# T1 = W22 - W12 formed by TensorE with an identity and a negated identity, in an f32 kernel of 64 conditioned 64x64 mixings and a routed 1024x1024 layer

## The reference

```python
W = weights[condition]
y = jnp.einsum('bct,bcd->bdt', x, W)
logits = y @ gate_w.T + expert_bias
one_hot = jax.nn.one_hot(jnp.argmax(logits, axis=-1), 4)
base_out = jnp.einsum('bth,oh->bto', y, W_up)
z = jnp.einsum('nh,erh->ner', y, lora_A)
d = jnp.einsum('ner,ehr->neh', z, lora_B)
out = x + base_out + jnp.einsum('neh,ne->nh', d, one_hot)
```

## Time and profile before

| | value |
|---|---|
| median of 3 runs | 405.35 us (405.1 to 405.51) |
| the profiled execution's own time | 405.92 us |
| its span in the trace | 404.1 us |
| TensorE (PE) busy | 398.5 us, 99% |
| VectorE (DVE) busy | 300.8 us, 74% |
| ScalarE (ACT) busy | 110.3 us, 27% |
| GpSimd (POOL) busy | 129.1 us, 32% |
| granted TensorE clock | 1.0 in the profile's row |

### The profile page before, as it was taken

The page is one execution under the profiler, slowest core; times in us unless marked ns, Lnnn a source line. Parts: engine busy times, 40 slices in busy tenths (PEclk is TensorE's granted clock), DMA queues, the critical chain, the costliest instruction groups (busy, mean ns, idle before and its releaser), DMA issues.

```text
span 404.1 us, 9748 instructions
## 1 busy us (share of the span) xinstructions
PE 398.5 (99%) x3451; PEld 358.3 (89%) x3451; DVE 300.8 (74%) x719; ACT 110.3 (27%) x226; POOL 129.1 (32%) x121
## 2 busy tenths in 40 slices
PE   8899999999999999999999999999999999999997
PEld 8899988989888898988979798898988889898996
DVE  3899668889876859676696766867677766967775
ACT  5896211323114031312213130130311203131310
POOL 1687302529031350505205080221605043050710
PEclk9999999999999999999999999999999999999999
DMA  7910330503214123413125032150332221250102
GB/s 255 350 62 2 122 101 28 190 27 113 87 66 145 53 87 105 133 55 113 50 78 187 28 109 68 49 177 26 110 104 93 95 79 58 104 182 27 54 32 99
DMA packets 20993, 39.39 MB, mean 97 GB/s; under 512 B 7494, under 2 KB 7750, under 8 KB 20970
## 3 DMA queue, kind: packets, MB, share of 16 engines
q1 hardware_dynamic: 17600, 27.40, 18.9%
q10 hardware_dynamic: 3370, 11.69, 9.3%
HBM read 22.30 MB, written 16.78 MB: 97 GB/s over the span
## 4 chain that ended last, share of the span: by engine, by line
PE 96%; DMA 1%; SPq 1%; ACT 1%; issue 0%; DVE 0%
PE bank_y L878 23%; PE bank_x L878 22%; PE bank_b L878 11%; PE bank_c L929 10%; PE y_ps L791 7%; PE bank_c L1083 5%; PE bank_b L1083 4%; PE bank_x L856 2%; DMA cond_pair<-in_L_cond_weights_dram 1%; PE bank_c L878 1%; PE bank_b L884 1%; PE bank_x L884 1%; PE bank_y L884 1%; PE bank_c L884 1%; PE bank_y L856 1%; PE y_ps L1157 1%
## 5 line engine op out<-in xcount | busy, mean ns | idle before, releaser
L878 PE MATMUL bank_y<-w_s,hl_s 128*128 128x292 f32 (+1 forms) x384 | 51.5, 290 | 0.0
L878 PEld LDWEIGHTS bank_y<-w_s,hl_s 128*128 128x128 f32 x384 | 49.2, 188 | 2.5 <-issue 2.5
L878 PE MATMUL bank_x<-w_a,hl_a 128*128 128x256 f32 (+1 forms) x384 | 50.8, 288 | 0.0
L878 PEld LDWEIGHTS bank_x<-w_a,hl_a 128*128 128x128 f32 x384 | 49.5, 188 | 0.4
L878 PE MATMUL bank_y<-w_a,hl_a 128*128 128x292 f32 x360 | 47.7, 288 | 0.0
L878 PE MATMUL bank_b<-w_s,hl_s 128*128 128x512 f32 x192 | 47.7, 397 | 0.0
L878 PEld LDWEIGHTS bank_y<-w_a,hl_a 128*128 128x128 f32 x360 | 46.6, 188 | 0.3
L307 POOL TENSOR_TENSOR s_sum<-a 128x512 f32<-128x512 f32 x9 | 11.6, 1287 | 105.5 <-DVE a L1405 102.4
L878 PE MATMUL bank_x<-w_s,hl_s 128*128 128x292 f32 x336 | 44.6, 289 | 0.0
L929 PE MATMUL bank_c<-w_s,hl_s 128*128 128x512 f32 x168 | 44.4, 410 | 0.0
L878 PEld LDWEIGHTS bank_x<-w_s,hl_s 128*128 128x128 f32 x336 | 43.1, 188 | 0.1
(11 more groups left out here) (193 smaller groups left out, 619.1 us busy)
## 6 DMA issues: line engine op xcount, KB each, us to landing
out_dram<-x_sb SPq DMA_DIRECT2D x63, 256.0 KB, 2.0
x_sb<-in_x_dram ACTq DMA_DIRECT2D x22, 512.0 KB, 3.6
x_sb<-in_x_dram SPq DMA_DIRECT2D x10, 512.0 KB, 3.4
w_raw<-in_L_ffn_W_up_dram SPq DMA_DIRECT2D x8, 512.0 KB, 5.8
cond_pair<-in_L_cond_weights_dram SPq DMA_DIRECT2D x64, 16.0 KB, 2.7
out_dram<-x_sb SPq DMA_DIRECT2D x2, 128.0 KB, 1.9
router_sb<-in_L_ffn_lora_A_dram ACTq DMA_DIRECT2D x1, 128.0 KB
lora_b_sb<-in_L_ffn_lora_B_dram SPq DMA_DIRECT2D x1, 128.0 KB, 5.2
```

The source lines that it names most:

```text
L878: mm = pe.matmul(dst, hl[op][:, a, k, :], w[:, b, k, cols], start=(fresh and k == 0 and a + b == 0), stop=(k == KH - 1 and a == 1), skip_g ...
```

## The change

T1 is no longer made of a transposed b12 that ScalarE copies and VectorE subtracts from. `form_t1(c)` stands where `turn("b12", c)` stood: for each of four 128-column pieces, one f32 matmul with the raw block of row 4 + c as the stationary operand and the identity as the moving one, and a second one with the raw block of row c and a negated identity, added in PSUM. ScalarE copies the sum to `t_sb` (`copy_t1`), VectorE's four `form_sum(1, c)` are gone. The negated identity is made by GpSimd in the place of `z_parts`, ahead of its other clears. The load of row 2 now waits for block 0's T1 in place of its b11, that of row 3 for block 1's T1. The expert bias is loaded by SyncE's queue behind x tile 2, not by ScalarE's queue at the start.

```diff
+        neg_ident = z_parts[:, :, :].rearrange("p n q -> p (n q)")
...
             def load_w_up(row):
                 c = row % OH
                 if c >= 2:
-                    for b in ("b11", "b21") if row < OH else ("b12", "b22"):
+                    for b in ("b21", "b12") if row < OH else ("b12", "b22"):
                         sp.wait_ge(piece_stage[b][c - 2], TURNED)
...
             load_first_pair(1, 0)
             sp.dma_start(x_sb[:, 2, :], x_pairs[2]).then_inc(x_loaded[2], 16)
+            sp.wait_ge(bias_zero, 1)
+            sp.dma_start(bias_sb[:, 0:E], expert_bias.rearrange("(a n) -> a n", a=1).to_broadcast([P, E]))\
+              .then_inc(bias_loaded, 16)
             load_first_pair(1, 1)
...
+            pool.memset(neg_ident, 0.0).then_inc(neg_zero, 1)
+            pool.wait_ge(neg_zero, 1)
+            pool.affine_select(out=neg_ident, in_=neg_ident, compare_op=ALU.not_equal, fill=-1.0,
+                               base=0, pattern=[[-1, P]], channel_multiplier=1).then_inc(neg_done, 1)
...
-            act.wait_ge(bias_zero, 1)
-            act.dma_start(bias_sb[:, 0:E], expert_bias.rearrange("(a n) -> a n", a=1).to_broadcast([P, E]))\
-                .then_inc(bias_loaded, 16)
...
-            def copy_b12(c):
+            def copy_t1(c):
                 act.wait_ge(piece_stage["b12"][c], TURNED)
-                act.activation(b12_sb[:, c, :], bank_of(("b12", c)), ACT.Copy).then_inc(piece_stage["b12"][c], 1)
+                act.activation(t_place(1, c), bank_of(("b12", c)), ACT.Copy).then_inc(t_stage[1][c], 1)
...
+            def form_t1(c):
+
+                pe.wait_ge(w_up_loaded[c], 16)
+                pe.wait_ge(w_up_loaded[OH + c], 16)
+                pe.wait_ge(neg_done, 1)
+                for k in range(KH):
+                    dst = bank_of(("b12", c))[:, k * P:(k + 1) * P]
+                    cols = slice(k * P, (k + 1) * P)
+                    pe.matmul(dst, w_raw[:, raw_slot(OH + c), cols], ident[:, :], start=True, stop=False)
+                    mm = pe.matmul(dst, w_raw[:, raw_slot(c), cols], neg_ident, start=False, stop=True)
+                mm.then_inc(piece_stage["b12"][c], 1)
...
                 else:
-                    pe.wait_ge(piece_stage[b][c], HIGH)
+                    pe.wait_ge(t_stage[1][c], FORMED)
...
-            turn("b12", 0)
+            form_t1(0)
...
             def form_sum(k, c):
-                if k == 1:
-                    dve.wait_ge(piece_stage["b12"][c], HIGH)
-                    dve.wait_ge(piece_stage["b11"][c], HIGH)
-                    a, b = b12_sb[:, c, :], bank_of(("b11", c))
-                elif k == 2:
+                if k == 2:
...
-            form_sum(1, 0)
```

More of the change, by code:

```diff
@@ L142, in adaln_ffn_kernel @@
         ident_done = sem("ident_done")
+        neg_zero = sem("neg_zero")
+        neg_done = sem("neg_done")
         zeros_done = sem("zeros_done")
@@ L629, in _ @@
             round_piece("b11", 0)
-            copy_b12(0)
+            copy_t1(0)
             round_piece("b22", 0)
@@ L638, in _ @@
             round_operand("a12", a12, 0, False)
-            copy_b12(1)
+            copy_t1(1)
             round_piece("b22", 1)
@@ L645, in _ @@
             round_operand("a11", a11, 0, False)
-            copy_b12(2)
+            copy_t1(2)
             round_sum(2, 1)
@@ L655, in _ @@
             round_piece("b11", 3)
-            copy_b12(3)
+            copy_t1(3)
             round_sum(2, 2)
@@ L951, in _ @@
             pe.wait_ge(gate_stage, LOW)
-            turn("b12", 1)
+            form_t1(1)
             wait_piece_read("b22", 0)
@@ L959, in _ @@
             wait_y_moved(0, 0)
-            turn("b12", 2)
+            form_t1(2)
             turn("b22", 2)
@@ L972, in _ @@
             wait_piece_read("b11", 1)
-            turn("b12", 3)
+            form_t1(3)
             wait_y_moved(1, 0)
@@ L1346, in _ @@
             low_piece("b21", 1)
-            form_sum(1, 1)
             low_piece("b22", 1)
@@ L1353, in _ @@
             form_sum(4, 1)
-            form_sum(1, 2)
             low_sum(dve, 3, 1)
@@ L1360, in _ @@
             low_piece("b11", 3)
-            form_sum(1, 3)
             low_sum(dve, 4, 0)
```

## The result

| | before | changed |
|---|---|---|
| median | 405.43 us (4 runs, 405.1 to 406.38) | 409.66 us (4 runs, 409.37 to 410.18) |
| ratio | | 1.0102, 95% interval 1.0081 to 1.0123 |
| span of the profiled execution | 404.1 us | 407.6 us |

The changed kernel is 4.2 us slower, and its traced span 3.5 us longer. The two differ because the traced execution of the kernel before (405.92 us) was 0.5 us over its median, and that of the changed kernel (409.40 us) 0.3 us under. The forecast was +3.9 us, 409.2 us.

What follows compares the result with a forecast made beforehand. TensorE bounds the kernel, with no listed wait after 14.95 us. 0.20 + 1.34 - 0.30 + 2.68 = +3.9 us on the median 405.35 gives 409.2 us; range 408.3 to 410.3.

Steps and rivals of the forecast that it cites:

- The price of T1: Each block's T1 on TensorE: eight plain matmuls, 1.78 us, replace four transposes, 0.44 us; +1.34 us a block.
- The factor of 4: Rival on T1's price by the skill's rule: T1 of 3.5 us, +3.04 us a block, 416 us; chance 0.01.
- Block 0: First T1 mostly hidden: the gate holds block 1's T1 until 12.19 us, not 11.99; 0.20 of 1.34 us left.
- Block 1: T1 paid in full, +1.34 us, less 0.30 of ScalarE's backlog; block 2's T1 starts at 16.17 us, +1.22.
- ScalarE's backlog: Ahead of block 2: copy of b12 and rounding of b22 in front of the move, 0.30 us, now done by 15.24.
- Blocks 2 and 3: Nothing waits any more before 35 us, so both T1s are paid in full: 2 x 1.34 = 2.68 us.
- Loads and bias: Later loads of `W_up` rows, x tile 3 and bias cost nothing; the bias has 1.3 us of cover.
- the rival with 0.10: Gate does not hold block 1: earlier loads count, block 1's T1 starts 0.6 us sooner; 408.6 us, chance 0.10.
- The rival of a faster kernel: VectorE paces the opening: four sums leave the path, extra TensorE work lies in gaps; 402.6 us, chance 0.03.

Runs made afterwards that it cites:

- The doubled kernel: Changed kernel with T1's eight matmuls done twice over in blocks 2 and 3; 413.91 us against 405.91 for the kernel before, ratio 1.0190.
- the two half-way kernels: Changed kernel with T1 on TensorE for blocks 0 and 1 only, 407.00 us, or 2 and 3 only, 407.44; kernel before beside them 405.91.
- no_t1_sums: Kernel before without VectorE's four T1 sums and with no added matmuls, T1 lacking its b11 part; 405.83 us against 405.94, ratio 0.9996.
- the repeat: The changed kernel run once more, unchanged; 409.74 us against 405.82 for the kernel before, ratio 1.0090.
- the last experiment: Kernel before with the bias late and x tile 1's load issued ahead of pair 1; 405.16 us against 405.92, ratio 0.9977.
- the late bias alone: Kernel before with only the bias's load moved to SyncE's queue behind x tile 2, run twice; 405.96 against 405.94 us, 405.94 against 405.82.

## Why the prediction was right

**The price of T1.** Taken from the first y's rows, 1.78 us; measured 1.78 to 1.89, the higher values where a wait stands in front. The doubled kernel gives 0.22 us a matmul again. The factor of 4 that the prediction took from the Trainium skill, "TensorE: Matmul & The Clock Gate", section Terms, would have made a T1 3.5 us long. The trace does not agree: a plain f32 matmul of this shape costs twice a transpose (0.22 against 0.11 us), not four times.

**Block 0.** Forecast: 1.14 of the 1.34 us hidden, block 1's T1 at 12.19, held by the gate. Measured 12.02, held by the gate, in the first trace and 12.47 in the second. The forecast took one start for T1 of block 0, 6.92 us; in fact it began at 6.65 and at 7.17, and the chain from it through copy, b22, T2 and gate carries that difference on. The chain itself was well sized: from T1 to block 1's T1 it took 5.37 and 5.30 us, forecast 5.27. That block 1's T1 was only 0.03 us later than before in the first trace, with 0.20 forecast, is luck with the start. In the kernel before it could not be seen, since TensorE then waited for the conditioning pair anyway.

**Block 1.** Forecast 16.17 us for T1 of block 2, with ScalarE's backlog worked off; measured 16.09 and 16.54. From block 1's T1 it is 4.07 us in both, 0.09 more than forecast, since a T1 with a wait in front costs 1.89 us and not 1.78. In the first trace this and the early start nearly cancel.

**Blocks 2 and 3.** Forecast 2 x 1.34 us in full. Block 3's b11 was due at 22.1, reckoned from the chain's 19.58; the changed kernel's chain has it at 21.98 (the timeline, which starts it earlier, 19.41 before and 21.82 now). From block 2's b12 or T1 to the mark it took 22.03 us before and 24.67 now, +2.64. With the 1.14 us in front that is the 3.78 us by which the mark moved, of the 3.9 forecast. Doubling the matmuls there confirms it, and so does the distance of the two half-way kernels.

**Loads and bias.** Row 3 was issued at 14.15 as worked out and nobody waited for it; the bias was 3.2 us on its way and stayed hidden. That the earlier loads are worth nothing as long as the gate holds block 1 was the forecast, against the rival with 0.10; putting the bias back cost nothing that could be measured.

**VectorE.** The rival of a faster kernel fell with no_t1_sums: it lost the same sums, and the time stayed.

The measured +4.2 us has an interval of +3.3 to +5.0 us, and the repeat gave +3.9; no term of the sum needs mending beyond the 0.1 to 0.4 us by which TensorE's early starts differ between executions.

What stays open: why the change of one load's place makes the last experiment faster in the median, how often x tile 1 is late, why the late bias alone gains nothing in the median, and the late wait for VectorE at 80 us in two kernels.

## What to carry to other kernels

Before moving work from a busy engine to another, ask which one waits: here VectorE was busy for 98% of a stretch and still nobody waited for it, while every matmul put on TensorE was paid, except in front of a wait that already stood there. A transposition with a plain f32 matmul and an identity costs twice a transposition in the transpose mode (0.22 against 0.11 us for 128x128), and the subtraction by a negated identity doubles it again (1.78 against 0.44 us for four). A gain in front of a load is only kept if the next load is in time too, so look for the next wait before counting it.

## What was not expected of the hardware

- The spread load of the bias, 2 KB in all, went with a slow stretch: from 7 to 9 us the queues moved 179 to 262 GB/s in the four traces that load it at the start, and 394 to 410 in the ten that load it late. In the kernels that begin with b12 as before, the first y started 0.4 to 1.8 us later with it (11.07, 11.01 and 10.55 against 10.14, 10.10, 9.68, 9.40 and 9.31 us).
- In the opening, TensorE's matmuls come at twice their later spacing up to some moment between 4.3 and 7.2 us, which differs between executions of one program (0.86 against 0.44 us for four transposes at the same place), while the granted clock in the profile's windows reads 1.00 there.
- One idle stretch of TensorE of 2.4 us within a busy opening was followed by a granted clock of 0.66 over four us.
